# A two-norm mixer-and-experts block on one core: weights that centre, sums by short products, a new hand-written order

## The reference, cut to what matters

```python
def block(x):
    u = ln_c(x)                                    # norm over the 64 channels, eps 1e-6
    zxbcdt = einsum('bhwc,oc->bhwo', u, W_in)      # 128 z, 128 x, 32 B and C, 8 dt
    dt = softplus(zxbcdt[..., 288:] + dt_bias)
    xBC = silu(depthwise_conv3x3(xBC) + conv_b)
    KV = B^T (xs * (dt * exp(A_log)))              # per image and head
    y = (C KV + xs * D) * silu(z)
    y = layernorm(y) * ln_g + ln_b                 # over 128 channels, eps 1e-5
    x = x + y W_out^T
    t = ln_t(x)                                    # norm over the 64 channels, eps 1e-5
    p = softmax(t gate_w + gate_b); keep the two largest of 8
    return x + sum_e p_e * (gelu(t W1_e + b1_e) W2_e + b2_e)   # all 8 experts, exact gelu
```

## Time and profile before

| what | value |
|---|---|
| times of three runs | 200.47, 200.51, 207.96 us |
| median | 200.51 us |
| span of the profiled execution | 206.1 us |
| mean granted TensorE clock | 0.904 |
| busy: TensorE, VectorE, ScalarE, GpSimd | 180.7, 117.1, 91.0, 66.2 us |

### The profile page before, as it was taken

How to read it: one execution, slowest core, us unless ns; L and a number is a source line. 1 busy time by engine, 2 the same in 40 slices (tenths; PEclk the granted TensorE clock), 3 DMA queues, 4 the chain that set the end, 5 groups by cost and what they waited for, 6 DMA issues and landing times.

```text
span 206.1 us, 2710 instructions
## 1 busy us (share of the span) xinstructions
PE 180.7 (88%) x885; PEld 81.1 (39%) x885; DVE 117.1 (57%) x307; ACT 91.0 (44%) x156; POOL 66.2 (32%) x82
## 2 busy tenths in 40 slices
PE   3969997999999989849999989989796999489970
PEld 1555345844365534426633426423233332122210
DVE  0255275467788895627399865993736923134350
ACT  2222015422653297642283276566263667234720
POOL 7060003000603000208204305424744244252883
PEclk9975797579999999985699999999999999958998
DMA  3217500000000004950002970003970029800004
GB/s 81 54 15 135 124 0 0 0 2 0 0 3 0 3 2 108 203 102 5 0 0 57 203 153 5 0 23 86 203 153 3 0 57 229 180 3 0 0 0 102
DMA packets 7559, 11.82 MB, mean 57 GB/s; under 512 B 3762, under 2 KB 6970, under 8 KB 7034
## 3 DMA queue, kind: packets, MB, share of 16 engines
q1 hardware_dynamic: 7546, 11.66, 26.2%
HBM read 10.48 MB, written 1.18 MB: 57 GB/s over the span
## 4 chain that ended last, share of the span: by engine, by line
PE 58%; DMA 13%; POOL 9%; issue 7%; DVE 7%; ACT 2%; POOLq 1%; SPq 0%; DVEq 0%; ACTq 0%
PE pm L895 13%; DMA gates<-cwd 11%; POOL acc L392 6%; PE pe L1011 5%; PE pe L1024 5%; PE pe L895 4%; PE pr L1028 3%; PE pm L881 2%; PE pm L858 2%; PE pr L969 2%; DMA cwd<-cwS 2%; PE pr L986 1%; PE pm L934 1%; PE pr L955 1%; PE pr L979 1%
## 5 line engine op out<-in xcount | busy, mean ns | idle before, releaser
L392 POOL TENSOR_TENSOR acc<-acc,tmp 128x512 f32<-128x512 f32 x28 | 35.4, 1272 | 43.4 <-DVE tmp L809 43.0
L517 ACT ACTIVATE hid<-pe,b1T 128x512 f32<-128x512 f32 x48 | 30.3, 682 | 22.5 <-PE pe L1011 22.4
L809 DVE SCALAR_TENSOR_TENSOR tmp<-pe,b2T,gates 128x512 f32<-128x512 f32 x24 | 18.0, 749 | 19.5 <-PE pe L1024 13.0
L1011 PE MATMUL pe<-fst,w 64*128 64x512 f32 x96 | 28.5, 671 | 0.5 <-ACT hid L517 0.4
L895 PE MATMUL pm<-pad,wT 64*128 64x512 f32 x108 | 27.2, 641 | 0.0
L1024 PE MATMUL pe<-hid,w 128*64 128x512 f32 x96 | 26.6, 632 | 0.2 <-DVE tmp L809 0.2
L376 POOL TENSOR_TENSOR rg<-ge,halves 128x8 f32<-128x8 f32 x4 | 6.8, 1708 | 43.0 <-DVE ge L766 43.0
L895 PEld LDWEIGHTS pm<-pad,wT 64*128 64x128 f32 x108 | 10.8, 201 | 14.5 <-issue 14.5
L541 DVE SCALAR_TENSOR_TENSOR bcc<-bcp,cw_bc,bcc 128x256 f32<-128x256 f32 x32 | 15.5, 484 | 1.0
L517 ACT ACTIVATE hid<-pm,b1T 128x512 f32<-128x512 f32 x16 | 10.1, 683 | 10.7 <-PE pm L1011 5.6
L809 DVE SCALAR_TENSOR_TENSOR tmp<-pm,b2T,gates 128x512 f32<-128x512 f32 x8 | 6.0, 751 | 14.7 <-PE pm L1024 10.1
(11 more groups left out here) (200 smaller groups left out, 280.3 us busy)
## 6 DMA issues: line engine op xcount, KB each, us to landing
gates<-cwd SPq DMA_DIRECT2D x8, 1024.0 KB, 9.5
xin<-in_x_dram SPq DMA_DIRECT2D x8, 128.0 KB, 3.5
out_dram<-acc SPq DMA_DIRECT2D x8, 128.0 KB, 2.4
w<-in_L_ffn_W_dram SPq DMA_DIRECT2D x3, 256.0 KB, 4.4
cwd<-cwS SPq DMA_DIRECT2D x4, 32.0 KB, 1.6
wx_raw<-in_L_conv_W_in_dram SPq DMA_DIRECT2D x1, 64.0 KB, 2.2
wz_raw<-in_L_conv_W_in_dram SPq DMA_DIRECT2D x1, 64.0 KB, 1.9
cw_bc<-in_L_conv_conv_w_dram SPq DMA_DIRECT2D x4, 1.1 KB, 1.8
```

Source lines behind the costliest of these rows:

```text
L392: pool.tensor_tensor(acc[p][:], (x2 if e == 0 else acc)[p][:], tmp[ln][e % 2][:], ALU.add).then_inc(summed[ln].sem, 1)
L517: act.activation(hid[ln][e % 2][:, q, :], expert_banks(g)[q][:], ACT.Gelu, bias=b1T[:, e:e + 1]).then_inc(hid_in[ln].sem, 1)
L809: dve.scalar_tensor_tensor(out=tmp[ln][e % 2][:], in0=expert_banks(g)[2][:], scalar=b2T[:, e:e + 1], in1=gates[p][:, e, :], op0=ALU.add, o ...
L1011: ins = pe.matmul(expert_banks(g)[q][:], w1[half, e, :], fst[p][half, :], start=True, stop=True)
```

## The change

- **Centring in the weights.** Each row of the input projection loses its mean over the 64 input channels before it is used (`wb`, `tap`, `wz`: a sum and a subtraction each on VectorE), so the product with an uncentred, scaled x is the centred one. The experts' W1 and the gate weights are multiplied by the centring matrix once (`wc0` to `wc2` on TensorE, `we0` to `we2` on ScalarE). The centring products and the copies of centred tiles go.
- **Sums from two short products.** `st` makes, from x with a 32-column stationary tile, the means and the dt projection, and from x squared the mean squares, in two 32-partition strips of one bank; ScalarE copies 34 rows (`cc`), TensorE transposes them in four pieces (`tt`), and VectorE makes the variance in four short operations (`moments`). `st2`, `tt2` do the same for the second norm, with the logits in the place of dt. `var`, `dt`, `v2` and `gt` go; the router starts from `tt2` and the power.
- **Softplus series on GpSimd.** `sp`: 13 dependent operations of 128x64. VectorE keeps `sf` (three) and `sg` (three).
- **To ScalarE:** `rx`, `rxg`, `rx2` (spreads), `bcp`.
- **Fillers:** 28 `busy` tokens for 12, and GpSimd writes their tile first.
- **Tables early:** one-column activations `tE`, `tS` that bring a table in ahead of its first use.
- **Four gate loads:** experts 0 to 3 and 4 to 7 are separate pairs of copies with a semaphore each; `m0` waits for the first pair, `m4` for the second.
- **Loads:** the three weight loads and two dt constants are issued by ScalarE. taps and the raw W1 share memory with gates[1].
- **Four buffers** for dt's tiles in the place of two, and a new PLAN.

```diff
 PLAN = """
+busy0 busy0 busy0 busy0 busy0 busy0 busy0 busy0 busy0 wt0 wb0 tap0 wn0 tE0 ea0 busy0 busy0 busy0 busy0 busy0
+busy0 busy0 busy0 busy0 busy0 busy0 busy0 busy0 busy0 st0 sq0 tT0 wz0 cc0 sq1 tt0 tU0 tV0 ve0 tf0
+te0 pw0 tg0 busy0 busy0 busy0 busy0 st1 rb0 dtv0 rx0 cc1 ex0 tt1 busy0 bd0 xn0 ve1 cv00 bcp0
+sf0 nm0 sp0 k00 cv10 k10 cv20 wc00 k20 pw1 sg0 tS0 bcs0 dtv1 xs00 rx1 z0 nT0 xs10 sz00
+xt00 sz10 xt10 rb1 we00 v00 bt0 v10 wc10 btc0 xn1 kv0 bd1 kvc0 ex1 sq2 sf1 y0 we10 wc20
+st2 cv01 y00 sp1 tt2 cc2 y10 sq3 bcp1 ne0 we20 k01 gs00 gs10 cv11 ps0 ve2 k11 pw2 sg1
+rx2 dtv2 stc0 c00 rb2 cf0 stt0 k21 ex2 cv21 bd2 xn2 tS0 bcs1 gst0 pj0 sf2 pwg0 xs01 bcp2
...
+z2 u00 y11 sz02 sz12 xt02 pj1 gs01 rt20 cwt0 gs11 sg2 bt2 xt12 cwc0 v02 btc2 ps1 gw0 pc1
+v12 stc1 kv2 stt1 kvc2 st3 gst1 h00 y2 pwg1 cc3 u10 y02 rxg1 h10 rbg1 d00 tt3 x21 u20
+st21 ve3 sq21 h20 m00 pw3 y12 d10 gs02 u30 cc21 a00 rx3 m10 h30 tt21 rb3 dtv3 d20 ve21
...
@@ sync
+                    for k in range(2):
+                        part = slice(E // 2 * k, E // 2 * k + E // 2)
+                        for q in range(2):
+                            sp.dma_start(gates[p][C * q:C * q + C, part, :],
+                                         cwd[p][E * q + part.start:E * q + part.stop, :].unsqueeze(0)
+                                         .broadcast_to([C, E // 2, HT])).then_inc(d_gate[k].sem, 16)
@@ gpsimd
+                elif step == "sp":
+                    pool.wait_ge(dt_dve.sem, dt_dve.at(g, 6))
+                    pool.tensor_tensor(dtq[g][:], dts[g][:], dts[g][:], ALU.mult).then_inc(c.sem, 1)
+                    after(1)
+                    pool.tensor_scalar(dtp[g][:], dtq[g][:], 1.0 / 13.0, 1.0 / 11.0, ALU.mult, ALU.add).then_inc(c.sem, 1)
+                    for k, m in enumerate((9, 7, 5, 3, 1)):
+                        after(2 + 2 * k)
+                        pool.tensor_tensor(dtp[g][:], dtp[g][:], dtq[g][:], ALU.mult).then_inc(c.sem, 1)
+                        after(3 + 2 * k)
+                        pool.tensor_scalar(dtp[g][:], dtp[g][:], 1.0 / m, None, ALU.add).then_inc(c.sem, 1)
+                    after(12)
+                    pool.tensor_tensor(dtp[g][:], dtp[g][:], dts[g][:], ALU.mult).then_inc(c.sem, 1)
@@ scalar
+                if step in ("tE", "tS", "tG"):
+                    act.activation(spare[:, 1:2], spare[:, 0:1], {"tE": ACT.Exp, "tS": ACT.Silu, "tG": ACT.Gelu}[step])
+                elif step == "rx":
+                    act.activation(r1w[p][:].rearrange("p (t c) -> p t c", c=C), bcast(r1[g], C), ACT.Copy).then_inc(wide.sem, 1)
@@ vector
+            def moments(msq, out, means, squares, eps, c, g):
+                dve.tensor_copy(out[:], means).then_inc(c.sem, 1)
+                dve.tensor_tensor(msq[:], out[:], out[:], ALU.mult).then_inc(c.sem, 1)
+                dve.scalar_tensor_tensor(out=out[:], in0=squares, scalar=eps, in1=msq[:],
+                                         op0=ALU.add, op1=ALU.subtract).then_inc(c.sem, 1)
+                dve.tensor_scalar(out[:], out[:], eps, None, ALU.max).then_inc(c.sem, 1)
@@ tensor
-                    pe.matmul(b0[:], centring[:], xin[g][:], start=True, stop=True).then_inc(cen.sem, 1)
+                    pe.matmul(b0[0:SC, :], stat_x[:], xin[g][:], start=True, stop=True)
+                    pe.matmul(b0[SC:2 * SC, :], onesb[:], sq[p][:], start=True, stop=True).then_inc(stat1.sem, 1)
+                elif step == "tt":
+                    for j in range(TJ):
+                        ins = pe.transpose(b1[:, SR * j:SR * j + SR], s1[p][:, P * j:P * j + P], ident[0:SR, 0:SR])
+                    ins.then_inc(turned1.sem, 1)
```

More of the change, by code:

```diff
@@ L18 @@
 PLAN = """
[L19 to L23, removed]
@@ L84, in two, with four @@
             return [sb(f"{name}{k}", shape, dt) for k in range(2)]
+        def four(name, shape, dt=f32):
+            return [sb(f"{name}{k}", shape, dt) for k in range(NG)]
         def sem(name):
@@ L146, in metaformer_block @@
         sz = two("sz", [P, 2, HT])
[L147 to L154, removed]
+        dtv = four("dtv", [P, NT, NH])
+        dta = four("dta", [P, NT, NH])
+        dtu = four("dtu", [P, NT, NH])
+        dtd = four("dtd", [P, NT, NH])
+        dts = four("dts", [P, NT, NH])
+        dtq = four("dtq", [P, NT, NH])
+        dtp = four("dtp", [P, NT, NH])
+        dA = four("dA", [P, NT, NH])
         bT = two("bT", [P, 2, GI, BC])
@@ L336, in _ @@
-            pool.wait_ge(i_pool, 5)
-            pool.tensor_tensor(centring[:], centring[:], ident[:], ALU.add).then_inc(i_pool, 1)
-            pool.memset(onesb[:], 0.0).then_inc(i_pool, 1)
-            pool.wait_ge(i_pool, 7)
-            for r in range(2):
-                pool.memset(onesb[C * r:C * r + C, r:r + 1], 1.0 / C).then_inc(i_pool, 1)
-            pool.wait_ge(i_pool, 9)
-            pool.memset(halves[:], -0.5).then_inc(i_pool, 1)
-            pool.memset(junk[:], 1.0).then_inc(i_pool, 1)
@@ new lines, in _ @@
+            pool.wait_ge(i_pool, 12)
+            made(pool.memset(wbc[:], 0.0))
+            made(pool.memset(spare[:], 1.0))
+            made(pool.memset(halves[:], -0.5))
+            made(pool.memset(gw[:], 0.0))
+            made(pool.memset(pad[0][:], 0.0))
+            made(pool.memset(bcp[0][:], 0.0))
+            made(pool.memset(pad[1][:], 0.0))
+            made(pool.memset(bcp[1][:], 0.0))
+            made(pool.memset(centring[:], 0.0))
+            pool.wait_ge(i_pool, 21)
+            for r in range(2):
+                made(pool.memset(centring[C * r:C * r + C, C * r:C * r + C], -1.0 / C))
@@ new lines, in _ @@
+            pool.wait_ge(i_pool, 23)
+            made(pool.tensor_tensor(centring[:], centring[:], ident[:], ALU.add))
+            for k in range(2):
+                made(pool.memset(bT[k][:], 0.0))
+            made(pool.memset(onesd[:], 1.0 / DI))
+            made(pool.memset(own[:], 0.0))
+            pool.wait_ge(i_pool, 28)
+            for i in range(GI):
+                made(pool.memset(own[BC * i:BC * i + BC, i % 2:i % 2 + 1], 1.0))
+            pool.wait_ge(i_pool, 32)
+            for e in range(E):
+                made(pool.memset(rank[:, e:e + 1], float(E - e)))
@@ L678, in steps @@
[L678 to L683 removed]
+                    dve.wait_ge(turned1.sem, turned1.at(g, 1))
+                    moments(msq1[g], ve[g], *summed_up(b1), 1e-6, var_eps, g)
@@ L716, in steps @@
                 elif step in ("k0", "k1", "k2"):
                     convolve(int(step[-1]), g)
-                elif step in ("sf0", "sf1"):
-                    softplus(int(step[-1]), g)
                 elif step in ("v0", "v1"):
```

633 lines of the change are left out of this document (332 added, 301 removed).

## The result

The changed kernel took 184.79 us (median of 4 runs, 182.36 to 185.19), against 202.55 for the kernel before in the same comparison (4 runs, 200.47 to 207.96). The ratio is 0.916, with a 95% interval of 0.905 to 0.927; disturbed executions are left out of it, so it isn't quite the ratio of the medians. Forecast were 179 us and 168 to 192.

A forecast was written before the change was run, and what follows sets the result against it. TensorE, busy 180.7 of 206.1 us, was taken as the skeleton, with holes and half-clock stretches. Sum: 206.1 - 4.2 - 4.3 - 20.4 = 177.2, plus 1.9 around the span, 179 us; range 168 to 192.

The forecast's parts named there:

- What stands around the span: Time outside the profiled span, added to the summed span at the end: 1.9 us.
- the half loads: At the gate holes of groups 0 and 3: first weighing starts some 4 us earlier, holes nearly close; 11.0 us credited.
- stage 3: From the first row of group 1 to the end, 163.3 us: gain 20.4 from products saved and gate holes.
- stages 1 and 2: Start to group 0's last convolution row, gain 4.2 us; then to the first row of group 1, gain 4.3.
- leave 2.8 for what remains: Gate holes with half clock behind, 13.8 us: 11.0 credited as won, 2.8 kept as still lost.
- the halves land together: Rival at gates of groups 0 and 3: four copies share engines evenly, m0 waits 11.4 not 7.1; 188 us, chance 0.08.
- 9.4 of products go: Beyond the start, both norms: 2 x 1.43 + 4 x 1.62 us of TensorE products saved, credited in full.
- about 7 later: Cover for the GpSimd softplus series after group 0, some 11 us there, about 7 later; so the series costs nothing.
- a sign that the forecast had named: Listed as showing the forecast wrong: TensorE idle in front of a transposed spread; no size given.
- slower: Rival: GpSimd series operations cost 1.7 us each, delaying the chain by 62 us: 241 us, chance 0.03.
- ScalarE gets in the way: Rival: each of 12 spreads waits behind a 1.28 us table load or activations, 15 us: 194 us, chance 0.08.
- the rival of half clock in 12 to 23 and 33 to 43: Fillers don't hold the clock, both early stretches stay low, 4.9 us each: 189 us, chance 0.17.

## Why the prediction was right, and where its parts were wrong

The verdict, the range and the direction held: 184.79 against 179, inside 168 to 192. What stands around the span was 2.1 us instead of 1.9. The parts came out otherwise, and that the total is within 6 us is in part luck: the start won 2.1 us more than forecast and the half loads some 2.5 more, which made up for about half of the 9.8 us by which the rest of stage 3 fell short.

**The start, stages 1 and 2: right, and a little better than forecast.** The profile gives 32.2 for the first row of group 1, where 34 was forecast: 10.6 us less than before, forecast 8.5. The first convolution ended at 23.56 (25.7), because `st0` began at 8.04 rather than 9.5: the fillers went at full pace from 4.91 on, where the forecast had the rise at 7.0. Most steps behind it have the forecast's prices (power 1.67, spread 0.64, norm 0.70); the spread's transpose took 0.67 against 0.45. But 9.6 of these 10.6 us are the lost clock of one execution of the kernel before. With full clock the old start has this row at 33.26. The forecast said so of the profiled trace, and only against that trace does the gain hold whole.

**The half loads: right mechanism, undersized.** Forecast 11.0; measured 13.5 by undoing them and, by adding them alone, 14.8 between medians and 12.7 to 15.5 between the executions at the highest clocks. m0 came at 76.0, forecast 75. VectorE's two long waits for gates, 9.5 us together in the kernel before, became 3.2. The step that failed is "leave 2.8 for what remains": the 13.8 us of the two holes and the half clock behind them went almost whole. The rival *the halves land together* fell: the load on the chain took 7.38 us, not 11.4.

**Products saved: the term that was mis-sized.** This is the step "9.4 of products go" in stage 3. The forecast took it one for one, since TensorE was the longest engine. Stage 3 was to win 20.4 us; by the traces it won 13.1 (163.3 to 150.2), which the half loads win alone (163.3 to 149.8). The product time fell by 6.4 us (its own lower clock included), the idle time rose by 6.8. Put back, 8.4 us of products cost 4.0. So the term is worth nothing to about half of its size: nothing by the pair of traces, half by the runs. Idle time that the rest of the change brought in, such as the series on GpSimd, is in the pair of traces too.

All that the change does beyond the half loads is worth little. Without them it is 2.6 us (the ratio 0.987). On top of them it is 3.6 between medians (188.41 to 184.79), but nothing that can be told against the three executions of the old order with half loads at a clock of 0.989 or 0.990 (184.99, 185.08, 185.42; the last two with eight fillers more). So the 3.6 would be mostly the clock that the other executions of the old order lose, in the one trace of such an execution between 23 and 43 us. In the changed kernel's trace these stretches are at 1.00. Why its order keeps the clock there, and whether it always does, isn't shown.

**The GpSimd series: mis-sized and not free.** The tile dtp in the changed kernel (duration in ns: shortest, median, longest):

```profile
L411 POOL TENSOR_TENSOR dtp<-dtp,dtq x20: 317/350/527, 17.3 to 102.8; 128x64 f32<-128x64 f32 x20
L413 POOL TENSOR_SCALAR dtp<-dtp x20: 367/482/1010, 17.9 to 103.2; 128x64 f32<-128x64 f32 x20
```

I took 0.33 an operation and 5.6 us a group with handovers; the page has means of 0.38 and 0.53 for these two lines, and the series on the chain takes 6.2 us (97.85 to 104.03), with nearly 0.08 between operations. The cover of "about 7 later" was too thin: in group 3 the series stands on the chain, and moving it back wins 2.2 by the medians. In group 1 the series also stood ahead of a power, that of group 2's first norm, and TensorE stood 0.88 us in front of the transposed spread at 40.08, a sign that the forecast had named. That costs nothing: with the series on VectorE this power starts at 38.90 instead of 37.68. The Trainium skill (GPSIMD Engine Reference, section 3, Performance versus the Vector engine) led to an estimated 0.44 an operation; it lies between the two means, mine below both. The rival *slower* needed 0.93 an operation and fell.

**Spreads to ScalarE: put at nothing, and they won about 2 us** that the sum didn't have. Their price was right by luck: the 0.67 of the earlier trace rows was a mean of 0.43 and one long one (below), and on ScalarE each took 0.61 to 0.63. The rival *ScalarE gets in the way* fell as worked out (every spread behind a table load, 194); what is left of it is the one place around 103 to 115.

**The fillers:** the rival of half clock in 12 to 23 and 33 to 43 fell: 1.00 through the first 66 us of the trace. But 28 were not needed: 12 gave 183.04.

**What stays open** is the hole at 103 to 119. Neither the series (2.2 us), nor ScalarE's order of `sz13` and `bcs3`, nor VectorE's load ahead of it explains it alone. The trace shows where it ends: ScalarE stands 3.97 us in front of the tanh of the router of group 2, and behind the tanh in its queue are the spread `rx22` and the GELU `h11` that TensorE waits for.

```profile
113.53 0.26 ACT L590 ACTIVATE th<-ld 128x64 f32<-128x64 f32 x1 [3.97 <-DVE ld L670]
113.69 0.61 ACT L585 ACTIVATE r2w<-r 128x512 f32<-128x512 f32 x1
114.21 1.25 ACT L605 ACTIVATE hid<-pe,b1T 128x512 f32<-128x512 f32 x2
```

A plan with `th2` behind `h11` would test that, and one with GpSimd's additions moved away from the router would test what the last section shows. Neither was tried.

## What to carry to other kernels

When a bulk load ends a wait, ask first which part of it the first consumer needs, and give that part its own copies and its own semaphore: here ten lines brought 13 to 15 of some 17 us. Products taken from the busiest engine count only in stretches where that engine is what ends last; before crediting them, look for the chain of small operations that runs beside them, since with the products gone that chain can be the bound. And a trace at a lowered clock shows a loss that another execution of the same kernel may not have: credit it once, and look at the spread of the runs for its size.

## What the runs showed that was not expected

**GpSimd and VectorE hold each other up.** The timeline of the changed kernel at the hole (start, length, engine, line, operation):

```profile
103.98 2.70 POOL L440 TENSOR_TENSOR acc<-acc,tmp 128x512 f32<-128x512 f32 x2
104.05 1.25 DVE L799 TENSOR_SCALAR dtv<-dtv 128x64 f32<-128x64 f32 x1 [1.72 <-POOL dtp L415]
...
105.33 0.23 DVE L801 SCALAR_TENSOR_TENSOR dtp<-dtp,dtv 128x64 f32<-128x64 f32 x1
105.59 1.17 DVE L806 TENSOR_TENSOR dA<-dtp,expA 128x64 f32<-128x64 f32 x1
```

GpSimd runs two additions of 128x512, 2.70 us together. The VectorE operation that starts during the first lasts 1.25 us, until about the middle of the 2.70; the next, at the turn from one addition to the other, takes its usual 0.23; the one after that lasts until about the end of the second. L665 and L670 at 111.0 and 112.3 (1.02 and 1.12 us) stand against two further additions in the same way. Four such stand on the chain through the hole, some 3.7 us beyond their usual time. Both router lines took this long in three groups, each time beside additions, and 0.23 in the first group, with none beside. `L659`, which reads one input from PSUM, took its 0.23 beside an addition (110.75). The Trainium skill (GPSIMD Engine Reference, section 1, Specifications) says that GpSimd's SBUF interfaces are shared with VectorE, with contention for VectorE instructions in a 2-port mode or with two SBUF inputs; the trace agrees and gives the size. In the other direction, GpSimd's 128x64 `L413` takes up to 1.01 us beside VectorE work (33.25, beside `L842`).

The kernel before had it too, in its spreads on VectorE. Three of four take 0.43 us; the fourth, at 146.53 on its chain, runs beside an addition of `L392` and takes 1.41, and `L793` at 155.99 does the same:

```profile
L771 DVE COPY rgw<-rg x4: 427/427/1410, 55.0 to 146.5; 128x512 f32<-128x512 f32 x4
```

That fits the 2 us that the spreads won on ScalarE, but no run separates it from VectorE's smaller load.

**The pace of products and the granted clock can differ at the start.** In the kernel with no fillers the granted clock is 1.00 in the first 12.2 us, as it is with fillers:

```profile
0.00:12.20 12.20, 5.33 (x19) 2.72 (x19) 4.72 (x14) 4.43 (x11) 7.09 (x45) 1.00 0.29 62
```

Yet its `st` product took 1.06 us against 0.55, and with fillers the first nine took 0.38 and the others 0.22. So at the very start the price of a known product tells the level, and a row at 1.00 may not. The row can fall there, as the 0.61 with 12 fillers shows.
